# A transformer layer kernel: another order in its opening, with the low parts of K on another engine and two score banks reduced by one instruction

## The reference

```python
xn = _layernorm(x, axis=-1)
q, k, v = (xn @ Wq), (xn @ Wk), (xn @ Wv)            # heads of 64
scores = jnp.einsum('bqhd,bkhd->bhqk', q, k) * SCALE
attn = jax.nn.softmax(scores, axis=-1)
out = jnp.einsum('bhqk,bkhd->bqhd', attn, v)
attention = out @ Wo + bo
logits = jnp.einsum('btd,ed->bte', xn, router_w)     # argmax picks the expert
h = jnp.square(jax.nn.relu(jnp.einsum('btd,edh->ebth', xn, expert_fc)))
out_e = jnp.einsum('ebth,edh->ebtd', h, expert_proj)
return x + attention + (out_e of the chosen expert)
```

## Time and profile before

| | |
|---|---|
| median of 3 runs | 1435.21 us (1434.1 to 1436.35) |
| the profiled execution | 1433.47 us |
| its span in the profile | 1431.7 us |
| TensorE busy | 1394.3 us (97%) |
| GpSimd busy | 1083.7 us (76%) |
| VectorE busy | 1163.4 us (81%) |
| ScalarE busy | 736.6 us (51%) |

### The profile page before, as it was taken

The page is one execution under the profiler, slowest core; times in us unless marked ns, Lnnn a source line. Parts: engine busy times, 40 slices in busy tenths (PEclk is TensorE's granted clock), DMA queues, the critical chain, the costliest instruction groups (busy, mean ns, idle before and its releaser), DMA issues.

```text
span 1431.7 us, 20036 instructions
## 1 busy us (share of the span) xinstructions
PE 1394.3 (97%) x6427; PEld 859.2 (60%) x6427; DVE 1163.4 (81%) x1543; ACT 736.6 (51%) x1314; POOL 1083.7 (76%) x858
## 2 busy tenths in 40 slices
PE   5899999999999999999999999999999999999996
PEld 3555666566656666656656666666665665656553
DVE  7889978888788788878788778887778788878865
ACT  4254555555545545555545554555555554545552
POOL 8279777767777767777777777777777777789996
PEclk8899999999999999999999999999999999999998
DMA  3423111321122211221113211133102231000000
GB/s 81 109 57 91 41 41 25 89 66 41 41 53 61 65 42 41 72 66 41 41 41 91 63 38 28 43 89 88 41 3 61 64 70 23 23 16 21 10 23 15
DMA packets 64967, 72.09 MB, mean 50 GB/s; under 512 B 8928, under 2 KB 38112, under 8 KB 64864
## 3 DMA queue, kind: packets, MB, share of 16 engines
q1 hardware_dynamic: 63840, 68.72, 19.4%
q0 software_dynamic: 1024, 2.10, 0.5%
HBM read 17.83 MB, written 5.11 MB: 16 GB/s over the span
## 4 chain that ended last, share of the span: by engine, by line
PE 87%; DVE 7%; issue 2%; POOL 2%; ACT 1%; SPq 1%; DMA 0%; POOLq 0%; DVEq 0%
PE OB L1024 28%; PE SB L996 16%; PE MB L1012 15%; PE SB L1000 14%; DVE mx L686 3%; PE XB L1061 2%; PE XB L1052 2%; PE XB L1070 2%; POOL acc L437 2%; PE XB L986 1%; PE XB L979 1%; DVE acc L702 1%; PE XB L1031 1%; PE XB L1033 1%; PE XB L1032 1%
## 5 line engine op out<-in xcount | busy, mean ns | idle before, releaser
L437 POOL TENSOR_TENSOR acc<-acc,ex 128x512 f32<-128x512 f32 x668 | 876.7, 1333 | 155.3 <-ACT ex L536 128.0
L536 ACT ACTIVATE ex<-SB 128x512 f32<-128x512 f32 x1024 | 608.1, 598 | 471.5 <-PE SB L1000 414.2
L686 DVE TENSOR_REDUCE mx<-MB 128x1 f32<-128x512 f32 x1024 | 683.4, 687 | 187.6 <-PE MB L1012 185.3
L1024 PE MATMUL OB<-ex,V 128*64 128x512 f32 x2048 | 466.1, 597 | 0.0
L996 PE MATMUL SB<-Q,K 128*128 128x512 f32 x1024 | 426.9, 417 | 0.0
L1012 PE MATMUL MB<-K,Q 128*128 128x512 f32 x1024 | 405.6, 400 | 7.0 <-DVE mx L686 6.2
L1000 PE MATMUL SB<-Q,K 128*128 128x512 f32 x1024 | 401.2, 392 | 1.6 <-DMA Q<-mrow 1.6
L702 DVE TENSOR_TENSOR acc<-acc,ex 128x512 f32<-128x512 f32 x228 | 287.8, 1262 | 30.2 <-POOL acc L437 19.7
L1024 PEld LDWEIGHTS OB<-ex,V 128*64 128x64 f32 x2048 | 138.4, 137 | 270.2 <-issue 238.2
L996 PEld LDWEIGHTS SB<-Q,K 128*128 128x128 f32 x1024 | 193.7, 189 | 139.0 <-issue 103.0
L1012 PEld LDWEIGHTS MB<-K,Q 128*128 128x128 f32 x1024 | 193.8, 190 | 58.8 <-DVE mx L686 16.5
(11 more groups left out here) (125 smaller groups left out, 567.3 us busy)
## 6 DMA issues: line engine op xcount, KB each, us to landing
Q<-qhi SPq DMA_DIRECT2D x124, 128.0 KB, 2.8
K<-khi SPq DMA_DIRECT2D x112, 128.0 KB, 2.3
Q<-qlo SPq DMA_DIRECT2D x64, 128.0 KB, 2.6
K<-klo SPq DMA_DIRECT2D x56, 128.0 KB, 2.3
w<-fc SPq DMA_DIRECT2D x23, 256.0 KB, 2.8
w<-projT SPq DMA_DIRECT2D x23, 256.0 KB, 3.6
sorted_x<-res SPq DMA_DIRECT2D x1, 1472.0 KB, 7.0
tok<-sorted_x SPq DMA_DIRECT2D x23, 64.0 KB, 1.8
```

The source lines that it names most:

```text
L437: pool.tensor_tensor(a[:, :], src[:, :], EX[h][ex_slot(kt)][:, :], ALU.add).then_inc(done, 1)
L536: act.activation(EX[h][ex_slot(kt)][:, :], SB[in_ring(2 * kt + h)][:, :], ACT.Exp).then_inc(a_e[h], 1)
L686: dve.tensor_reduce(mx[:, m % 2, u:u + 1], MB[in_ring(i)][:, :], AX.X, ALU.max).then_inc(v_m, 1)
L1024: mm = pe.matmul(OB[own[h], :], V[(n // JB) % 2][:, k, own[h]], EX[h][ex_slot(k)][:, :], start=(k == 0), stop=(k == NT - 1))
```

## The change

- TensorE makes Q of block 0 first, and then K of the four chunks. Each product has its bank: Q in MB[2], K in OB, SB[2], MB[2] and OB.
- VectorE no longer takes the low parts of K. ScalarE, after the two high parts of a chunk, copies the whole product from the bank to an `ex` buffer, and GpSimd subtracts the high part from this copy (`low_k0` is now on GpSimd, two instructions of 64x512 a chunk).
- The maxima of block 0 are taken in 16 pairs: two matmuls into two banks side by side, one reduction over both (`max_pair`, `maxima_pair`). Two pairs of banks alternate.
- The rows of ones in K2 are written by four DMAs from the tile `ones` instead of four GpSimd memsets. SP issues them once GpSimd has filled all zeros (`g_z`).
- VectorE does `rows` of chunk 0 before the statistics of chunk 1, and `rows` of chunk 3 after the low part of Q.
- Three max units of block 1 run ahead of `turn_max` instead of none.

```diff
-        BETWEEN = {3: ("v", 0), 7: ("v", 1), 11: ("v", 2), 15: ("v", 3), 19: ("q", 1),
-                   21: ("r", 0), 23: ("r", 1), 25: ("r", 2), 27: ("r", 3)}
-        START = [SB[0], SB[1], OB, XB]
-        TX = [MB[0], MB[1], MB[2], SB[2]]
+        BETWEEN = {1: ("v", 0), 3: ("v", 1), 5: ("v", 2), 7: ("v", 3), 8: ("q", 1),
+                   9: ("r", 0), 10: ("r", 1), 11: ("r", 2), 12: ("r", 3)}
+        TX = [SB[0], SB[1], MB[0], MB[1]]
+        START_Q, START = MB[2], [OB, SB[2], MB[2], OB]
+        PAIR = [a[:, 0:2 * QB] for a in (MB_all, SB_all)]
+        EARLY = 3
...
+                    sp.wait_ge(g_i, 5)
+                    sp.wait_ge(g_z, 4 + 2 * JB)
+                    for h in range(2):
+                        for k in range(2):
+                            sp.dma_start(K2[k][h][maxrow[h], :].bitcast(F32), ones[0:NT, :]).then_inc(d_one, 16)
                     sp.wait_ge(d_q0, 32)
                     sp.wait_ge(a_q0, 1)
                     sp.sem_inc(d_q[0], QD)
...
-                    sp.wait_ge(v_k, JB)
+                    sp.wait_ge(g_k0, 2 * JB)
...
+                def low_k0(c):
+                    q = slice(c * QB, (c + 1) * QB)
+                    pool.wait_ge(a_k, c + 1)
+                    for h in range(2):
+                        pool.tensor_tensor(K2[0][h][own[h], q], EX[0][c][own[h], :], K1[0][h][own[h], q], ALU.subtract)                            .then_inc(g_k0, 1)
...
-                    ins.then_inc(a_k, 1)
+                    ins.then_inc(a_k0, 1)
+                    act.activation(EX[0][c][:, :], START[c][:, :], ACT.Copy).then_inc(a_k, 1)
...
+                def maxima_pair(p):
+
+                    u = ORDER[2 * p]
+                    dve.wait_ge(t_m, 2 * p + 2)
+                    dve.tensor_reduce(mx[:, 0, u:u + JB + 1:JB], PAIR[p % 2].rearrange("p (a k) -> p a k", a=2), AX.X,
+                                      ALU.max).then_inc(v_m, 2)
...
-                    for s_ in range(1, JB + 3):
...
+                    low_w(Lin(0))
+                    statistics(2)
+                    rows(1)
+                    statistics(3)
+                    rows(2)
+                    low_q0()
+                    rows(3)
+                    for p in range(UNITS // 2):
+                        maxima_pair(p)
...
+                def max_pair(p):
+
+                    wait(pe, v_m, 2 * p - 2)
...
+                    for u in range(EARLY):
+                        max_unit(Lin(1), u)
                     turn_max(Lin(0))
-                    for u in range(LEAD):
+                    for u in range(EARLY, LEAD):
                         max_unit(Lin(1), u)
```

More of the change, by code:

```diff
@@ L322, in spread_k @@
                     k, q = pair % 2, slice(c * QB, (c + 1) * QB)
-                    wait(sp, v_k, pair.times(JB, c + 1))
+                    wait(sp, v_k, pair.times(JB, c + 1 - JB))
                     for h in range(2):
@@ L488, in first, with zero @@
                     pool.wait_ge(g_i, 6)
[L491 to L494, removed]
+                    k_zeros, q_zeros = ([t[h][other[h], :] for t in ts for h in range(2)] for ts in (K2, Q2))
+                    def zero(z):
                         pool.memset(z.bitcast(F32), 0.0).then_inc(g_z, 1)
[L496 to L505, removed]
+                    for z in k_zeros[:2] + q_zeros[:2]:
+                        zero(z)
+                    pool.wait_ge(g_z, 4)
+                    low_x(0)
+                    pool.wait_ge(g_lo, 1)
+                    for z in q_zeros[2:4]:
+                        zero(z)
+                    pool.wait_ge(g_z, 6)
+                    low_x(1)
+                    pool.wait_ge(g_lo, 2)
+                    low_k0(0)
+                    pool.wait_ge(g_k0, 2)
+                    low_x(2)
+                    pool.wait_ge(g_lo, 3)
+                    low_k0(1)
+                    pool.wait_ge(g_k0, 4)
+                    low_x(3)
+                    pool.wait_ge(g_lo, 4)
+                    low_k0(2)
+                    low_k0(3)
+                    pool.wait_ge(g_k0, 2 * JB)
+                    for z in q_zeros[4:] + k_zeros[2:]:
+                        zero(z)
+                    pool.wait_ge(g_z, 4 + 2 * JB)
                     pool.wait_ge(d_c, 32)
@@ L629, in first @@
                     act.activation(up[:, 0:1], eps[:, 0:1], ACT.Sqrt)
[L631 to L644, removed]
+                    root(0)
+                    split_w(Lin(0))
+                    root(1)
+                    turned(0)
+                    root(2)
+                    turned(1)
+                    root(3)
+                    high_q0()
+                    high_k0(0)
+                    turned(2)
+                    high_k0(1)
+                    turned(3)
+                    high_k0(2)
+                    high_k0(3)
                     copy_q0()
-                    for u in range(UNITS):
+                    for u in range(UNITS // 2):
                         if u in BETWEEN:
@@ L843, in first @@
                     statistics(0)
+                    rows(0)
                     statistics(1)
-                    for s_ in range(1, JB + 3):
[L846 to L861, removed]
+                    low_w(Lin(0))
[7 more added lines that the diff above has]
+                        maxima_pair(p)
+                        if p in BETWEEN:
+                            kind, c = BETWEEN[p]
                             if kind == "q":
```

68 lines of the change are left out of this document (38 added, 30 removed).

## The result

The changed kernel takes 1439.84 us (median of 7 runs, 1438.5 to 1440.37). The kernel before, run beside it, takes 1434.69 us (7 runs, 1434.1 to 1436.89). The ratio is 1.0031, with a 95% interval of 1.0019 to 1.0042: slower, by 5.15 us between the medians (the ratio, 0.31%, is 4.4 us). The forecast was +2.0 us with "no change that can be told" as the likeliest answer, and 1439.6 us for the rival in which the clock falls with the first logits. That rival is what happened. Its time was right to 0.2 us, but that is partly luck: its change was +4.4 us, where the medians differ by 5.15 and the traces by 5.2 to 5.3, and it stood on a median of 1435.21 for the kernel before, which was 1434.69 in the runs beside the changed kernel.

The account below looks back on a forecast made before the run. VectorE's reductions bound the prologue before, GpSimd's work after; TensorE is busy 97% of the span. Second scores matmul 1.0 late, clock in logits 0.7, block 0 0.3: +2.0 us, median 1437.2, range 1433.0 to 1441.0.

Parts of the forecast that it names:

- no change that can be told: Whole kernel: a median within 0.2%, 2.9 us, of before, 1432.3 to 1438.1; chance 0.57.
- the rival in which the clock falls with the first logits: Block 1's routing logits: TensorE's clock drops as they begin, slowing three groups and three pairs; +4.4 us, 1439.6; chance 0.25.
- The start: Opening, up to Q and K of chunk 0: V(1) held by GpSimd for 1.3 us; ScalarE's copy done at 18.2.
- GpSimd becomes the chain: Opening: GpSimd's subtractions for K, 1.27 us each, low parts of x and memsets set the pace; zeros end at 37.8.
- rival at half price: GpSimd's 64x512 subtractions cost 0.63 us each, as cost goes with rows; -1.8 us, 1433.4; chance 0.08.
- SP: SP's queue: four issues of ones take 2.8 us before raising d_q[0]; first logits at 42.1, 1.25 late.
- What VectorE saves is used up here: VectorE before the first logits: pairs start later, nine take 10.4 us, then a 1.3 us wait for Q of block 1.
- From logits to maxima: First logits to negated maxima: TensorE's 1.36 us pace exceeds a pair's 1.15; maxima at 52.8, late by 1.7.
- The clock: TensorE's lower clock in the logits and block 0: 0.7 us (0 to 3.1) plus 0.3 (0 to 1).
- I expect it to fall at the same place: TensorE's clock during the logits drops where it did before, catching one more group and pair; 0.7 us.
- The tail: Negated maxima to second scores matmul: 5.15 us instead of 5.84, a gain of 0.7; matmul late by 1.0.
- the copy, once hidden, becomes the last: Before the second scores matmul: units done by 4.5 us behind the maxima, so the copy landing at 5.15 ends last.

Follow-up runs that it names:

- e1: Changed kernel, but SP raises d_q[0] before it waits for GpSimd's zeros and issues the ones; 1434.82 us, 1.0005 of the kernel before.
- e3: Changed kernel with SP's raise of d_q[0] ahead of the ones and GpSimd's low parts of x before those of K; 1431.64 us, 0.9981 of before.
- e4: Changed kernel with fourteen unused matmuls of 512 columns filling TensorE's idle stretch ahead of Q of block 1; 1437.05 us, 1.0016 of before.
- e5: e3 with block 0's maxima taken by 32 single reductions instead of 16 pairs; 1434.80 us, 0.9997 of the kernel before.
- e6: e3 with no max units of block 1 ahead of the transpose of the maxima, instead of three; 1432.56 us, 0.9987 of before.
- e7: Changed kernel with K's low parts back on VectorE, without GpSimd's subtractions and ScalarE's copies, SP's order kept; 1433.48 us, 0.9991 of before.
- e11: Kernel before with only block 0's maxima in 16 pairs and the change's places for the other work; 1433.59 us, 0.9992 of before.
- e2: Changed kernel, but GpSimd makes all four low parts of x before its subtractions for K; 1440.27 us, 1.0039 of the kernel before.
- e10: Kernel before with one unused matmul of 512 columns behind each max unit of block 0 from the 21st on; 1434.68 us, 0.9999 of before.
- e9: e3 with logits in their own bank, spread over the pairs, and two unused matmuls behind each pair from the tenth; 1431.17 us, 0.9971 of before.

## Why the prediction missed by 3 us

- **"The start"** was right. V(1) took 2.11 us, while an undisturbed one of the same timeline took 1.11: held for about 1.0, where 1.3 was taken. V of chunk 3 was held too (3.14 us, beside GpSimd's first pair of subtractions), off the chain. The Trainium skill's rule of the shared port (SBUF — State Buffer, "Who interferes with whom") agrees with these rows; no experiment here takes the hold away by itself.
- **"GpSimd becomes the chain"** was right in route and size. A subtraction of 64x512 took 1.27 us, to the digit; low_x(3) started at 24.92 (24.6), the last zeros ended at 38.45 (37.8). The rival at half price is out. Of the 0.65 us, 0.3 were there at low_x(3) and 0.5 at the first of the last memsets (32.49 instead of 32.0); these took 6.0 with their gaps instead of 5.8.
- **"SP"**: 2.86 us for the four issues (2.8), raise at 41.48 (40.6), logits at 42.93 (42.1). Late by 2.07 instead of 1.25; e1 shows that this queue is the cause.
- **"What VectorE saves is used up here"** was right in the changed kernel: it waited 2.78 us instead of 1.3. A pair came every 1.13 us (1.15 taken). In e3 the wait ahead of qlo is down to 0.51 us, and the saving shows.
- **"From logits to maxima" and "The clock"** are where it failed. The forecast had 10.7 us from the first logits to nm and 0.7 for the clock on top; it was 14.42. From the first logits to `choose` 8.96 us passed instead of 5.65 (42.1 to 47.75): first group 1.25 instead of 1.06, three groups at 1.51 instead of 0.79, three pairs at 1.05 instead of 0.57. From there to nm it was 5.46 instead of 5.05, since the last pair's matmuls took 1.24 and VectorE waited 0.25 more. In sum 3.7 against 0.7. The sentence "I expect it to fall at the same place" failed: it fell three us sooner after the logits began. The idle stretch of 3.2 us ahead of them did that in this kernel, since filling it moves the fall back to 3.3 us (e4), though in e5 it fell 1.0 us behind them without such a stretch. The prediction named this as the argument for the rival, and had the idle time at "2 us or so". The rival's own sum was too low as well: +4.4 against the +5.2 of the traces. The logits came 0.8 later than it had, its price between logits and nm was 0.6 low (pairs at 0.86, measured 1.05, above all), and the tail and block 0 gave back 0.65. That its 1439.6 met the median is luck: it started from a median that was 0.5 too high.
- **"The tail"**: 4.80 us instead of the 5.15 forecast and the 5.84 before. The gain was 1.04, not 0.7; e6 measures 0.9 to 1.05. That "the copy, once hidden, becomes the last" at 5.15 isn't what the trace shows. The weight load ahead of the second scores matmul did wait for it:

```profile
61.99 0.29 PEld L1023 LDWEIGHTS SB<-Q,K 128*128 128x128 f32 x1 [0.37 <-DMA Q<-mrow]
```

But it started 4.64 behind nm, and the matmuls around it follow each other every 0.43 us (61.72, 62.15, 62.59), the pace of a matmul of 512 columns at the low clock, without idle time on TensorE. The copy came just in time, and the units and their clock set the 4.80.

- **"The clock", block 0**: 0.1 us instead of 0.3.

The sum: 0.83 (logits later) + 3.72 (logits to nm) - 0.35 (tail) - 1.0 (the 0.7 and 0.3 already in the forecast) = 3.2 us, which is the difference between +2.0 and the +5.2 of the traces.

What stays open: why the clock falls when it does. Behind the first logits it fell after 0.7 us in the changed kernel (3.21 us idle ahead), after 3.3 in e4 (0.64) and 3.9 before (0.91), but with 0.95 or 0.94 us idle ahead after 1.0 (e5), 2.3 (e7), 2.4 (e1, e3), 3.2 (e6) and 3.3 (e11), and in e2, with 7.26 us idle, it was at 0.50 before they began. These are single executions. They show that the fall moved with the idle stretch in one pair of kernels, and that something else moves it by more than 2 us where the idle time is the same. Also open is the rest of the kernel: the time behind the second scores matmul was 1374.5 to 1376.3 us over these kernels, with a lower granted clock at the very end (1400 to 1436 us: 0.86 before and after, 0.81 in e7, 0.79 in e10) where it was longer. Differences of about 1 us between medians shouldn't be read as effects of the opening alone.

## What to carry to other kernels

When work moves from the engine at the bound to an idle one, follow the idle engine's list to its end and ask which queue waits behind it: here a raised semaphore stood behind four transfers that stood behind six memsets, and moving three lines of SP's list was worth 4 to 5 us. An edit that is worth nothing alone may be worth 3 us beside another that removes the wait which swallows it. Price a stall on TensorE at two rates: its length, and what the matmuls behind it cost at the lower clock if another engine waits for them there; where none did, holding the clock high gained nothing here (e9, e10).

## What was not expected of the hardware

- A reduction over two banks side by side (128x1024 into 128x2) takes 1.21 to 1.23 us and the next starts 1.13 us later, so a pair saves 0.09 us over two single ones, 0.61 apart, and the nine ahead of the logits 0.8. Yet the logits came 3.6 us earlier in e11, of which the table gives 1.2, and e3 lost 3.2 us without them: the rest lies in waits and in the clock (e5), not in VectorE's pace.
- GpSimd needs 1.26 to 1.28 us for a subtraction of 128x512 and for one of 64x512. The Trainium skill (GPSIMD Engine Reference, "Instruction dispatch") has each core work on its own 16 partitions, and these rows agree: half the rows saved nothing.
- TensorE's records show it as busy for the whole of a stretch of logits (2.00 of 2.00 us), and the granted clock still falls to 0.50 there. Between the groups lie two matmuls of 512 columns; with two more such matmuls in each gap it stays at 1.00 (e10; e9 is alike).
- The same small issue on SP took 0.59 us three times and 0.96 (changed) or 1.43 us (e4) once.
